# A decoder's last stage: the second batch's plain projections placed in round 0, context values in round 1, and three heads' keys computed with the gates

## The reference, cut to what matters

```python
x = _layernorm(x + _L1_attn_ref(x, w_qkv, w_o))          # 16 heads of 32, causal: "plain"
x = _layernorm(x + _L1_xattn_ref(x, mask, ctx, ctx, wq, wk, wv, wo))   # one head over 512: "cross"
x = _layernorm(x + _L1_ffn_ref(x, W_gate, W_qkv))        # "shared"

# _L1_ffn_ref
gating = softmax(x @ W_gate.T)                  # 16 gates a token
indicator = one_hot(argmax(gating), 16)
q, k, v = split(x @ W_qkv.T, 3)                 # k, v as 16 heads of 32
k_shared = einsum('bth,bthd->btd', indicator, k)            # the chosen head's key
v_shared = einsum('bth,bthd->btd', indicator * top1, v)
y = causal attention of q's 16 heads over k_shared, v_shared
```

## Time and profile before

| | us |
|---|---|
| median of 3 runs | 2275.7 |
| profiled execution | 2275.38 |
| its span | 2273.6 |
| TensorE busy | 2116.7 (93%) |
| VectorE busy | 1231.6 (54%) |
| GpSimd busy | 589.0 (26%) |
| ScalarE busy | 517.4 (23%) |

### The profile page before, as it was taken

The page is one execution under the profiler, slowest core; times in us unless marked ns, Lnnn a source line. Parts: engine busy times, 40 slices in busy tenths (PEclk is TensorE's granted clock), DMA queues, the critical chain, the costliest instruction groups (busy, mean ns, idle before and its releaser), DMA issues. The chain is left out here.

```text
span 2273.6 us, 29273 instructions
## 1 busy us (share of the span) xinstructions
PE 2116.7 (93%) x11864; PEld 1231.1 (54%) x11872; DVE 1231.6 (54%) x1861; ACT 517.4 (23%) x783; POOL 589.0 (26%) x544
## 2 busy tenths in 40 slices
PE   6899999888999899799999878999999999999996
PEld 4444444233444476456666646566666666666653
DVE  2467777667999841022222234355757575747456
ACT  1444444430000121111111112122222222222221
POOL 1122222227888405011110311212121212111112
PEclk9999999989999899899999989999999999999997
DMA  9840000005111146811221510101010101000000
GB/s 174 96 40 29 29 29 19 31 19 191 41 46 41 51 152 113 230 65 66 67 67 61 205 69 29 47 1 47 1 56 1 57 1 38 3 27 10 1 10 19
DMA packets 66762, 129.63 MB, mean 57 GB/s; under 512 B 7450, under 2 KB 20968, under 8 KB 66632
## 3 DMA queue, kind: packets, MB, share of 16 engines
q1 hardware_dynamic: 44952, 75.43, 13.1%
q10 hardware_dynamic: 14976, 33.69, 5.3%
q0 software_dynamic: 6704, 18.64, 2.8%
HBM read 96.38 MB, written 41.85 MB: 61 GB/s over the span
## 5 line engine op out<-in xcount | busy, mean ns | idle before, releaser
L925 PE MATMUL conv_conv<-kv,toep 128*128 128x512 f32 x576 | 248.9, 595 | 4.6 <-POOL kv L946 4.6
L2223 DVE RECIPROCAL tail_inv<-tail_ring 128x256 f32<-128x256 f32 x64 | 112.4, 1756 | 181.6 <-PE tail_ring L1691 181.4
L1393 PE MATMUL moe_gu_ps<-gu,moe_xT 128*128 x624 | 199.6, 463 | 3.4 <-issue 1.8
L925 PEld LDWEIGHTS conv_conv<-kv,toep 128*128 128x128 f32 x576 | 110.0, 191 | 144.2 <-issue 136.1
L946 POOL TENSOR_TENSOR kv<-vT,cT 128x512 f32<-128x512 f32 x128 | 160.5, 1275 | 48.7 <-PE conv_conv L925 38.9
L1393 PEld LDWEIGHTS moe_gu_ps<-gu,moe_xT 128*128 128x128 f32 x624 | 116.3, 192 | 72.8 <-issue 23.6
L1968 POOL TENSOR_TENSOR tail_rstd_x<-tail_rstd_x,const_minus_half 128x2 f32<-128x2 f32 x32 | 22.6, 707 | 482.1 <-DVE tail_rstd_x L2175 482.1
L1975 POOL TENSOR_SCALAR_AFFINE_SELECT tail_expT<-tail_expT 128x1024 f32<-128x1024 f32 x64 | 70.4, 1100 | 288.6 <-ACT tail_expT L2045 288.1
L540 POOL TENSOR_SCALAR_AFFINE_SELECT front_expT<-front_expT 128x2048 f32<-128x2048 f32 x32 | 64.4, 2012 | 259.8 <-ACT front_expT L598 259.8
L1475 DVE TENSOR_TENSOR moe_hid<-moe_gu_ps,moe_silu 128x352 f32<-128x352 f32 x39 | 20.5, 525 | 179.4 <-PE moe_gu_ps L1393 179.4
L2045 ACT ACTIVATE tail_expT<-tail_scores 128x1536 f32<-128x1536 f32 x64 | 92.8, 1451 | 76.4 <-PE tail_scores L1669 76.4
(11 more groups left out here) (335 smaller groups left out, 4035.7 us busy)
## 6 DMA issues: line engine op xcount, KB each, us to landing
toep<-toeplitz SPq DMA_DIRECT2D x32, 320.0 KB, 2.8
y_slots<-moe_y ACTq DMA_DIRECT2D x39, 256.0 KB, 2.0
gu<-in_L_ffn_gate_up_proj SPq DMA_DIRECT2D x5, 1408.0 KB, 10.5
toeplitz<-filt_rows SPq DMA_DIRECT2D x1, 6144.0 KB, 67.2
front_e<-in_ctx SPq DMA_DIRECT2D x8, 512.0 KB, 5.6
toeplitz<-filt_rows SPq DMA_DIRECT2D x2, 2048.0 KB, 89.9
x_after<-x SPq DMA_DIRECT2D x8, 512.0 KB, 5.1
tail_x<-x_after SPq DMA_DIRECT2D x8, 512.0 KB, 3.8
```

Source lines behind the costliest of these rows:

```text
L925: ins = pe.matmul(bank, toep[p][:, mat * P:(mat + 1) * P], kv[p][:, c].rearrange("p b j i -> p (b j i)"), start=n == 0, stop=n == len(PART ...
L1393: ins = pe.matmul(gu_ps[:, s % 2, h, 0:HID], xT[:, c, :], wgu[c][:, e, h * HID:(h + 1) * HID], start=c == 0, stop=c == NC - 1)
L2223: link.after(dve.reciprocal(inv[c % 2][:], bank[:, S:2 * S]))
```

## The change

- Rounds 0 and 1 of all engines but GpSimd and SP are written out, and the loop starts at round 2. In round 0 each score of batch 0 stands behind the product that it needs, and the turn and the six q, k and v products of batch 1 stand between the shift, the transposed scores and the weighings of batch 0. They are kept in buffers that are free then: q in the shared attention's q, k in the second x5 buffer, v in the third.
- In round 1 batch 1 has only scores and weighing left. Batch 0's cross products stand between them. The first context value of batch 7 stands at the end of round 0, ahead of the output product, the second in round 1 behind the first score.
- VectorE's sum of the experts of batch 2 moves from the start of round 1 to behind the split of batch 1. At the end of round 1 the last mix moves behind the norm of x3 and the statistics of x5.
- The wait of ScalarE for the four stores is split in two semaphores, one for each batch.
- The weights of the gates lie ahead of those of the keys in one tile of 528 columns. The gates' product covers 112 columns: 16 gates and three heads' keys. The keys' product covers the other 416. VectorE copies all 224 columns (two row blocks) out and multiplies the keys in two pieces. The weights of the gates are loaded after the last context value, with the keys'.

The diff, cut to its core:

```diff
-        wide["gk"] = st.sb("gk", [P, NC, D])
+        wide["gk"] = st.sb("gk", [P, NC, NG + D])
+        gated = allowed[:, 2, 0:NT * (NG + LED * HD)].rearrange("p (t n) -> p t n", t=NT)
+        gate, led = gated[:, :, 0:NG], gated[:, :, NG:NG + LED * HD]
+        q_of = {1: qT["A"]}
+        k_of = {1: x5[1][:].rearrange("p t (c s) -> p (t c) s", s=S)}
+        v_of = {1: x5[2][:]}
...
                 def gates(b):
                     bank = ring.claim(pe, ("H", "g", b))
+                    n = NG + LED * HD
                     for t in range(NT):
-                        ins = project_rows(pe, bank[:, t * NG:(t + 1) * NG], xT[b % 2], t, wide["wgate"], 0, NG)
+                        ins = project_rows(pe, bank[:, t * n:(t + 1) * n], xT[b % 2], t, wide["gk"], 0, n)
+                def shared_keys(b, t):
+                    bank = ring.claim(pe, ("H", "k", b, t))
+                    project_rows(pe, bank[:, 0:D - LED * HD], xT[b % 2], t, wide["gk"], NG + LED * HD, NG + D)...
...
+                turn("P", "x3", 0)
+                turned("P", 0)
+                cols("P", "q", 0, 0, wide["wq"])
+                cols("P", "k", 0, 0, wide["wk"])
+                score("P", 0, 0)
+                cols("P", "q", 0, 1, wide["wq"])
+                score("P", 0, 1)
+                cols("P", "k", 0, 1, wide["wk"])
+                score("P", 0, 2)
+                rows("P", "v", 0, 0, xT[0], wide["wv"])
+                score("P", 0, 3)
+                rows("P", "v", 0, 1, xT[0], wide["wv"])
+                turn("P", "x3", 1)
+                turned("P", 1)
+                cols("P", "q", 1, 0, wide["wq"])
+                shift("P", 0)
+                cols("P", "k", 1, 0, wide["wk"])
+                scoreT("P", 0, 0)
+                cols("P", "q", 1, 1, wide["wq"])
+                scoreT("P", 0, 1)
+                cols("P", "k", 1, 1, wide["wk"])
+                weigh("P", 0, 0)
+                scoreT("P", 0, 2)
+                rows("P", "v", 1, 0, xT[1], wide["wv"])
+                weigh("P", 0, 1)
+                scoreT("P", 0, 3)
+                rows("P", "v", 1, 1, xT[1], wide["wv"])
+                weigh("P", 0, 2)
+                weigh("P", 0, 3)
+                ctx_values(B - 1, 0)
+                for t in range(NT):
+                    rows("P", "o", 0, t, mixedT, wide["wo"])
+
+                score("P", 1, 0)
+                ctx_values(B - 1, 1)
+                turn("C", "x4", 0)
+                turned("C", 0)
+                rows("C", "v", 0, 0, xT[0], wvo)
+                score("P", 1, 1)
+                rows("C", "v", 0, 1, xT[0], wvo)
+                score("P", 1, 2)
+                cols("C", "q", 0, 0, wa)
+                score("P", 1, 3)
+                cols("C", "q", 0, 1, wa)
+                shift("P", 1)
+                cross_scores(0, 0)
+                scoreT("P", 1, 0)
+                cross_scores(0, 1)
+                scoreT("P", 1, 1)
+                weigh("P", 1, 0)
+                cross_turn(0, 0)
+                scoreT("P", 1, 2)
+                weigh("P", 1, 1)
+                cross_turn(0, 1)
+                scoreT("P", 1, 3)
+                cross_out(0, 0)
+                weigh("P", 1, 2)
+                cross_out(0, 1)
+                weigh("P", 1, 3)
+                for t in range(NT):
+                    rows("P", "o", 1, t, mixedT, wide["wo"])
+
+                for r in range(2, B):
...
-                    if H_: turned("H", h); rows("H", "k", h, 0, xT[h % 2], wide["gk"]); gates(h)
+                    if H_: turned("H", h); shared_keys(h, 0); gates(h)
...
             def _(sp):
-                load("wgate")
...
-                for k in ("gk", "gv", "gq"):
+                for k in ("wgate", "gk", "gv", "gq"):
...
             def _(dve):
+                maxima("P", 1, 0)
+                norm("x4", 0)
+                for n in range(1, 4):
+                    maxima("P", 1, n)
+                split_top("P", 1)
+                experts_sum(2)
+                cross_max(0, 0)
+                cross_max(0, 1)
+                mix("P", 1, 0)
+                mix("P", 1, 1)
+                link.after(dve.reciprocal(xinv[:], xsum[:]))
+                cross_rows(0, 0)
+                mix("P", 1, 2)
+                cross_rows(0, 1)
+                norm("x3", 2)
+                statistics("x5", 0)
+                mix("P", 1, 3)
+                add_plain(1)
```

More of the change, by code:

```diff
@@ L1553, in tail_stage @@
         fetched = st.sem("fetched")
-        late_stored = st.sem("late_stored")
+        late_stored = [st.sem(f"late_stored{n}") for n in range(2)]
         ctxq_loaded = [st.sem(f"ctxq_loaded{p}") for p in range(2)]
@@ new lines, in _ @@
+                pe.wait_ge(loaded["wo"], 16)
+                for n in range(NC):
+                    drained(("P", "W", 0, n))
+                for t in range(NT):
[7 more added lines that the diff above has]
+                rows("C", "v", 0, 1, xT[0], wvo)
@@ L2079, in _ @@
+                exps("P", 1, 2)
+                take(("C", "p", 0, 1), probT[:, 1].rearrange("p k q -> p (k q)"))
+                exps("P", 1, 3)
+                for r in range(2, B):
                     p, c, h, a = (r - n if 0 <= r - n < B else None for n in range(4))
@@ L2277, in pick, with add_plain, cross_rows @@
                         link.after(ins)
+                def add_plain(b):
+                    for t in range(NT):
+                        key = ("P", "o", b, t)
+                        ins = add_rows("P", "o", "x4", "x3", b, t)
+                        ins.then_inc(ring.drained_sem(key), 1)
+                    dve.wait_ge(ring.drained_sem(key), ring.count(key))
+                    statistics("x4", b)
+                def cross_rows(b, t):
+                    key = ("C", "w", b, t)
+                    dve.scalar_tensor_tensor(out=buf("x5", b)[:, t, :], in0=filled(key), scalar=xinv[:, t:t + 1],
+                                             in1=buf("x4", b)[:, t, :], op0=ALU.mult, op1=ALU.add).then_inc(ring.drained_sem(key), 1)
                 dve.wait_ge(made, 2)
@@ L2281, in _ @@
                 norm("x3", 0)
-                for r in range(B):
+                experts_sum(1)
+                maxima("P", 0, 0)
+                norm("x3", 1)
+                for n in range(1, 4):
+                    maxima("P", 0, n)
+                split_top("P", 0)
+                for n in range(4):
+                    mix("P", 0, n)
+                add_plain(0)
+                maxima("P", 1, 0)
+                norm("x4", 0)
+                for n in range(1, 4):
+                    maxima("P", 1, n)
[5 more added lines that the diff above has]
+                mix("P", 1, 1)
+                for t in range(NT):
+                    key = ("C", "s", 0, t)
+                    dve.wait_ge(ring.drained_sem(key), ring.count(key))
+                link.after(dve.reciprocal(xinv[:], xsum[:]))
+                cross_rows(0, 0)
+                mix("P", 1, 2)
+                cross_rows(0, 1)
+                dve.wait_ge(ring.drained_sem(("C", "w", 0, 1)), ring.count(("C", "w", 0, 1)))
+                norm("x3", 2)
+                statistics("x5", 0)
+                mix("P", 1, 3)
+                add_plain(1)
+                for r in range(2, B):
                     p, c, h, a = (r - n if 0 <= r - n < B else None for n in range(4))
```

131 lines of the change are left out of this document (88 added, 43 removed).

## The result

The kernel after takes **2255.43 us** (median of 5 runs, 2251.38 to 2258.64); the kernel before, timed on the same chip, 2275.7 (2269.55 to 2280.37). The span of the profiled execution is 2249.2 against 2273.6. TensorE was busy for 2100.1 of it, 93% in both, and its mean granted clock is 0.972 against 0.966.

The account below looks back on a forecast made before the run. TensorE was taken to bound the kernel, with the score chain binding rounds 0 and 1. 2275.4 less 10.2 (gates) and 7.6 (rounds 0 and 1) is 2257.6, the median 0.3 above: 2258 us, range 2249 to 2267.

Parts of the forecast that it names:

- What bounds: Middle rounds: TensorE work without holes, so time taken off shortens the span; first two rounds: bound by the score chain.
- Round 0: Its pieces on TensorE sum to 71.6 us, ending at 1366.8, 2.6 later, with 23.4 of round 1's work done.
- Round 1: Waits of 2.6, 3.3 and 4.9 us; ends at 1433.2 at full clock, 15.5 less than before.
- The clock: Half-speed stretches behind round 1's three waits cost 2.5, 3.6 and 1.8, together 7.9 us (0 to 12).
- the clock holds: Rival: the clock does not drop at round 1's waits of 2.6 and 3.3; 2250 us, chance 0.2.
- The gates: Gate matmuls stay at 1.7 us with 112 columns; 416-column keys save 1.28 per batch, 10.2 over eight batches.
- The rival built on that: Weight loads add to the columns in the gates, giving +1.8 in place of -10.2; 2270 us, chance 0.07.
- VectorE: Copying 224 columns and multiplying keys in two pieces adds 0.8 us, at most 1.9, nothing on the path.
- Queues: Gate weights load later, ahead of batch 2's x rows on SP; margin 5 us, price nothing.
- The rival of late rows: Batch 2's x rows delay experts' sum and weighing; eight over margin gives 2266 us; chance 0.13, including similar overlooked waits.
- The low clock stays: Rival: TensorE stays at 1.2 GHz from round 1's first wait to round 2; 2290 us, chance 0.03.
- All given back at the end of round 1: Rival: round 0 is filled but its gain is lost again, only 10.2 remains; 2265 us, chance 0.07.

Follow-up runs that it names:

- rounds_only: Kernel after with the old gates (16 columns), leaving only the new order of rounds 0 and 1; 2268.26 us, 0.9963 of the kernel before.
- gates_only: Kernel before with the new gates alone, on the old order of rounds 0 and 1; 2265.2 us, 0.9952 of the kernel before.
- led7: Kernel after with seven heads' keys in the gates' product in place of three (240 columns, 288 left for the keys); 2260.03 us, one run.
- best4: best3 with four heads' keys in the gates' product in place of three (144 columns, 384 left); 2234.09 us, 0.9809 of the kernel before.
- fetch_late: Kernel after with GpSimd's four fetches of batch 3 moved behind the four masks of batch 1; 2249.19 us, one run.
- best3: Kernel after with the edits of fetch_late and weigh_swap, and the norm of x4 ahead of the first maxima; 2243.72 us, 0.9847 of the kernel before.
- weigh_swap: Kernel after with batch 1's last weighing ahead of the second cross output, last mix ahead of the second cross row; 2249.27 us, one run.

## Why the prediction was right, step by step

**The total.** The forecast took 17.8 off the profiled execution; the median came out 20.3 lower, and the profiled execution alone 24.4. Of these 24.4, 12.7 are rounds 0 and 1 (7.6 forecast), 9.7 the gates (10.2 forecast), 4.2 a gain at the end that was not forecast, and 2.2 a loss ahead of the stage that was not forecast either. The mechanism was right; that the median lies only 2.6 us from the forecast is partly luck.

**What bounds.** Right. TensorE is dense from round 2 on, and what left a dense round left the span: the period of a dense round went from 112.08 (1610.97 to 1723.05, before) to 110.88 (1599.26 to 1710.14, after), 1.20 less, as much as keys and gates lost.

**Round 0.** The sum was 71.6 from the first product on. Measured: 1297.36 to 1368.78, 71.4, with no low clock.

**Round 1.** Forecast e+22.4 for the end of score 3; measured 22.2 (1368.78 to 1390.98). From there 44.0 at full clock; measured 47.2 (to 1438.17), of which about 3.3 is clock: 1.8 in the output product (8.80 against 7.0) and half of a stretch of 3.4 behind 1409. The three waits were put at 2.6, 3.3 and 4.9, and were 2.30, 3.29 and 4.67. Most of the 0.3 by which the first came out smaller is in the add and the statistics ahead of it on VectorE: 2.5 from the end of round 0 (1368.78 to 1371.29), where 2.7 was reckoned.

**The clock.** This is the term that was mis-sized, and it has no single value: 7.9 forecast, 3.3 in the first trace of after, 7.1 in the second. The second hit the forecast's round 2 "near 1441" (1441.77). The first ended 3.8 earlier, on the side of the rival "the clock holds". A fall behind each wait was the right picture, but only as one of several outcomes of the same program. Wait by wait: behind the first 2.5 was forecast, and it cost nothing in the first trace and 2.8 in the second; behind the second 3.6, and it cost 1.5 and 2.5; behind the third 1.8, and it cost 1.8 in both.

**The gates.** Forecast 10.2, measured 1.21 by eight = 9.7. I take the gates of a dense round as the first product (keys and gates) less the second (keys alone), the same way in both kernels: 5.21-3.54 = 1.67 before and 4.64-2.90 = 1.74 after, 0.104 and 0.109 for a record. So the floor was nearly flat, as forecast. Each keys' product saved 0.64 (3.54 to 2.90), 1.28 together as worked out, and the gates took back 0.07 of it. The 1.85 of the group that stands alone doesn't show a higher floor: at another place near the end 16 columns (rounds_only, 2185.90 to 2187.95) and 112 columns (gates_only, 2183.12 to 2185.17) both take 2.05 at full clock. The Trainium skill, "TensorE: Matmul & The Clock Gate", Part 3, The mechanism, would have a load overlap running matmuls "only when row_grp differs". The rows of led7 do not agree: all records there use the full array, each with its own load, and 240 columns cost 0.201, their columns alone. The rival built on that is refuted.

**VectorE.** Costed at nothing on the path, and it was: the copy of 224 columns took 0.39, the two multiplies 0.26 and 0.58, and VectorE is busy for 61.8 of 112. No new wait stands in a dense round.

**Queues.** The x rows were in time. The experts' sum began at 1394.95, directly behind the split on VectorE, with no wait for a DMA; the small load of the gate weights, whose price was open, landed after 1.8 us, and the x rows after 7.8. The rival of late rows fell with that.

**What was not forecast: about 4 us at the end.** From round 2 on the gain was 13.9, and the gates explain 9.7. Near the end TensorE waits 2.2 for a norm in both kernels. Stretches around that wait, first before, then after:

```profile
2107.00:2123.00 16.00, 13.08 (x71) 9.18 (x70) 8.97 (x22) 1.40 (x3) 0.91 (x1) 0.68 0.00 0
```

```profile
2082.00:2100.00 18.00, 15.03 (x90) 9.12 (x89) 12.42 (x30) 1.68 (x4) 1.62 (x2) 1.00 0.00 0
```

Behind the same wait the kernel before ran at a mean of 0.68, and the kernel after at full clock. From round 2 to the end 36.8 us ran at 1.2 GHz before and 27.4 after. Taking half of that off as lost, an estimate that counts TensorE as busy throughout, leaves 806.5 before, 796.9 in gates_only and 797.3 after. The gates' 9.7 are all there, and the rest is clock. In both traces of before the stretch at 1.2 GHz behind that wait was 10.2 us long, in both of after 0. In rounds_only, gates_only and led7 it was 6.8, in best4 3.4, in fetch_late 0. Kernels with the same instructions at this place thus differ (best3 has 6.8 like led7, fetch_late and weigh_swap have 0), so the new gates alone don't set it. What decides whether a wait of this length is followed by a fall stays open; no run isolates it.

**The other rivals.** "The low clock stays" is refuted by 6.8 to 17 us at 1.2 GHz in rounds 0 and 1. "All given back at the end of round 1" is refuted by rounds_only, 8.4 us with an interval that excludes 0.

## What to carry to other kernels

Filling one round's holes with the next round's products pays in full only where the next round keeps cover of its own. After such a move, look at every engine for what stands ahead of the item that the critical engine waits for: here maxima ahead of a norm, four fetches ahead of a mask, a norm and statistics ahead of a mix, together 10.3 us of waits, and three small reorderings took 8.1 of it and the clock's loss as well. Narrow matmuls cost a floor for each record, so give them columns from a neighbour with the same input up to the width where the columns pass the floor (here between 112 and 144), and not beyond.

## What the runs showed of the hardware that was not expected

- The same program with the same waits (2.3, 3.3, 4.7) had 6.8 us at 1.2 GHz in one execution and 17.0 in another. The stretches at 1.2 GHz in rounds 0 and 1 lasted 3.4 to 17.1 us. With no wait above 1.3 behind the first product of the stage there was none from 1281 us to 2085 (best3).
- Every one of the sixteen single waits of 3.1 us or more in rounds 0 and 1 of the fourteen profiles (3.1, 3.3, 4.0 and 4.7) had a stretch at 1.2 GHz that began in it or right behind it. For the wait of 2.3 that is so in five of seven profiles, for the wait of 2.2 near the end in nine of fourteen.
- An fp32 matmul record, taken as the first product less the second over 16, costs 0.104 us at 16 columns (5.21-3.54, before), 0.109 at 112 (4.64-2.90, after), 0.121 at 144 (4.61-2.68, best4) and 0.201 at 240 (5.26-2.05, led7): a nearly flat floor and then the columns, with little in between.
- The multiply of 96 columns on VectorE took 0.26 us in the first row block (1494.86) and 1.06 in the second (1500.86). GpSimd was running an add then (1500.54, 1.27 long), and the multiply ended 0.1 behind it. The same holds for the only other slow one of the sixteen (1.27 at 2183.00, beside an add from 2182.89 to 2184.16); the fourteen others took 0.25 to 0.26, and none began while a GpSimd instruction ran. TensorE does not wait for it.
